# Waits between the four scatter rounds of the expert stages, on GpSimd's queue

## What is computed

```
x = x + attn_a(layernorm(x))      # state-space heads, 32 of them
x = x + ffn(layernorm(x))         # shared expert + 16 experts, top 4
x = x + attn_b(layernorm(x))      # gated linear attention, 16 heads
x = x + ffn(layernorm(x))         # the same weights again
```

```
shared = silu_and_mul(x @ shared_gate_up_w.T) @ shared_down_w.T
shared = shared * sigmoid(x @ sgate_w.T)
routing_weights = softmax(x @ gate_w.T)
topk_w, topk_ids = top_k(routing_weights, 4)
for e in range(16):
    coef = sum(where(topk_ids == e, topk_w, 0), axis=-1)
    h = silu_and_mul(x @ w13[e].T)          # 2 x 176 hidden columns
    acc = acc + (h @ w2[e].T) * coef[:, None]
out = shared + acc
```

## Time and profile before

| | us |
|---|---|
| runs, median of 3 | 1252.41 (1249.12 to 1254.31) |
| the profiled execution, its own time | 1253.93 |
| its span, first to last instruction | 1252.0 |
| TensorE matmul busy | 1175.0 (94%) |
| VectorE busy | 807.0 (64%) |
| ScalarE busy | 752.3 (60%) |
| GpSimd busy | 600.4 (48%) |
| scatters (L1285), 64 | 63.9 busy |
| scatter-adds (L1291), 88 | 137.6 busy |

### The profile page before, as it was taken

How to read it: one execution, slowest core, us unless ns; L and a number is a source line. 1 busy time by engine, 2 the same in 40 slices (tenths; PEclk the granted TensorE clock), 3 DMA queues, 4 the chain that set the end, 5 groups by cost and what they waited for, 6 DMA issues and landing times.

```text
span 1252.0 us, 23038 instructions
## 1 busy us (share of the span) xinstructions
PE 1175.0 (94%) x7484; PEld 1008.6 (81%) x7484; DVE 807.0 (64%) x2038; ACT 752.3 (60%) x1734; POOL 600.4 (48%) x497
## 2 busy tenths in 40 slices
PE   6999999999897899989999999999999989489997
PEld 5878888888784777768999999999999988377775
DVE  7766767777882433477777777777777787143335
ACT  5866667666551333427888887887888865033332
POOL 3211222121137165625776777677776643705663
PEclk9999999999997899989999999999999998789999
DMA  3366766653245777741322222232222015556665
GB/s 114 88 181 169 175 174 174 170 162 71 58 153 203 181 137 137 129 103 51 89 77 59 59 61 65 61 70 79 59 75 59 17 48 158 201 168 112 117 116 145
DMA packets 94277, 141.59 MB, mean 113 GB/s; under 512 B 8184, under 2 KB 73976, under 8 KB 93048
## 3 DMA queue, kind: packets, MB, share of 16 engines
q1 hardware_dynamic: 74400, 102.32, 29.8%
q0 software_dynamic: 15744, 20.98, 9.8%
q10 hardware_dynamic: 4056, 17.30, 4.6%
HBM read 99.71 MB, written 40.86 MB: 112 GB/s over the span
## 4 chain that ended last, share of the span: by engine, by line
PE 80%; DVE 6%; DMA 6%; issue 4%; ACT 2%; POOL 1%; SPq 0%; DVEq 0%; ACTq 0%; POOLq 0%
PE ps L276 20%; PE ps L278 19%; PE ps L277 19%; PE ps L1116 7%; PE ps L1141 5%; DMA sums_d<-e_y,xg 3%; PE ps L551 2%; DMA rows_a<-a_rows_d 1%; PE ps L1129 1%; PE ps L1093 1%; DVE valT L762 1%; PE ps L1680 1%; PE ps L565 1%; DMA a_vg_raw<-a_vg 1%; DVE x L1419 1%
## 5 line engine op out<-in xcount | busy, mean ns | idle before, releaser
L1291 POOL DMA_INDIRECT sums_d<-e_y,xg x88 | 137.6, 1564 | 137.2 <-ACT e_y L1218 79.8
L1116 PE MATMUL ps<-w,e_xT 128*128 (+1 forms) x376 | 127.2, 461 | 2.5 <-ACT e_xT L1201 1.7
L1412 DVE COPY e_hT<-ps 88x256 f32<-88x256 f32 x94 | 39.5, 420 | 132.0 <-PE ps L1129 118.0
L427 POOL TENSOR_TENSOR aw_lo<-aw_raw,aw_hi 128x512 fp32r<-128x512 f32 x32 | 42.0, 1317 | 152.5 <-ACT aw_hi L423 152.5
L276 PE MATMUL ps<-xn_hi,aw_hi 128*128 128x512 f32 x256 | 111.2, 434 | 2.7 <-DVE bmat_lo L790 2.7
L857 DVE TENSOR_TENSOR m_a<-ps,e_a 128x384 f32<-128x384 f32 x128 | 71.3, 557 | 58.5 <-PE ps L551 57.9
L278 PE MATMUL ps<-xn_hi,aw_lo 128*128 128x512 f32 x256 | 101.4, 396 | 0.0
L277 PE MATMUL ps<-xn_lo,aw_hi 128*128 128x512 f32 x256 | 100.9, 394 | 0.0
L1141 PE MATMUL ps<-w,e_hT 88*128 (+1 forms) x376 | 96.7, 379 | 0.0
L656 ACT COPY late<-ps 128x256 f32<-128x256 f32 x128 | 47.7, 373 | 69.7 <-PE ps L278 69.6
L427 POOL TENSOR_TENSOR ms_b_lo<-m_b,ms_b_hi 128x384 fp32r<-128x384 f32 x64 | 65.0, 1017 | 49.2 <-ACT ms_b_hi L423 49.2
(11 more groups left out here) (311 smaller groups left out, 4145.8 us busy)
## 6 DMA issues: line engine op xcount, KB each, us to landing
rows_a<-a_rows_d SPq DMA_DIRECT2D x64, 256.0 KB, 5.1
xg<-slots_d SPq DMA_DIRECT2D x94, 144.0 KB
slots_d<-slot_init SPq DMA_DIRECT2D x10, 1152.0 KB, 6.9
w<-moe_up ACTq DMA_DIRECT2D x8, 1408.0 KB
wconv_raw<-b_conv SPq DMA_DIRECT2D x16, 513.0 KB
aw_raw<-a_heads SPq DMA_DIRECT2D x32, 256.0 KB, 3.0
wvo_raw<-b_vo SPq DMA_DIRECT2D x16, 512.0 KB, 3.4
rows_b<-b_rows_d SPq DMA_DIRECT2D x32, 256.0 KB, 4.8
```

The source lines that it names most:

```text
L427: return nc.gpsimd.tensor_tensor(dst[1], src, f32(dst[0]), ALU.subtract).then_inc(sem(done_sem), 1)
L1116: ins = nc.tensor.matmul(ps[:, 2 + t % 2, 0:2 * E_HIDDEN], e_xT[:, t % 2, k], weights_of(w13, t, at_w, k * 2 * E_HIDDEN, 2 * E_HIDDEN), st ...
L1291: nc.gpsimd.indirect_dma_start(sums_d[f][t % CHAINS], bass.IndirectOffsetOnAxis(ap=xg[:, t % XG, ROW_ID:ROW_ID + 1].bitcast(U32), axis=0), ...
L1412: nc.vector.tensor_copy(e_hT[0:HALF_E, t % 2], ps[0:HALF_E, 4 + t % 2, 0:2 * P].rearrange("p (j m) -> p j m", j=2)).then_inc(sem("e_hT"), 1)
```

## The change

In both expert stages GpSimd waits, ahead of each round after the first, until all eight scatters of the round before have landed.

```diff
             for i, k in enumerate(reversed(range(TOP_K))):
+                if i > 0:
+                    pool.wait_ge(sem(f"slots_stored{i - 1}"), 16 * BLOCKS * (f + 1))
                 for b in range(BLOCKS):
                     if i == 0 and b % CHUNK_BLOCKS == 0:
                         routed(pool, "dve", f, f"slots{b // CHUNK_BLOCKS}")
```

## The result

| | before | after |
|---|---|---|
| runs beside each other, median of 11 each, us | 1252.41 | 1243.15 |
| ratio of after to before, 95% interval | | 0.9929 [0.9909, 0.9949] |
| the profiled execution, its own time, us | 1253.93 | 1240.95 |
| its span, us | 1252.0 | 1239.1 |

Faster, by 0.7%: 9 us by the runs, 13.0 us between the two profiled executions. The forecast was a gain of 18.5 us, to 1234 us.

The account below looks back on a forecast made before the run. TensorE's slow instruction flow during unbroken scatter bursts was taken as the bound. Tile 3 earlier by 7.5 + 15 us, less 4 for the clock, gives 18.5; 1253.9 - 18.5 - 1.5 = 1234 us, eight-in-ten range 1225 to 1260.

Parts of the forecast that it names:

- The slow stretches and their cure: Both expert stages, 25 and 28 us of slow matmuls inside the scatter burst: bursts of eight end them; chance 0.52, 1234 us.
- tile 3 waits for its load: Sign in the profile after: tile 3's turn waits for its load, at 418 to 423 and 1105 to 1110.
- The rival that the slow pace stays: TensorE is slowed by scatters under way, not their number in a row; stretches end 6.1 us later, 1262 us; chance 0.19.
- no change: Rival: pauses put off the slow pace's onset by about what they lengthen the burst; 1247 to 1258 us; chance 0.18.
- The price of the waits: GpSimd's three waits per stage: 3.7, 1.2 and 1.2 us added, 6.1 us in all, up to 4.5 more for weights.
- the forecast's own sum: Tile 3 starts earlier by 7.5 and 15 us in the two stages, less 4 for the clock: 18.5 us gained.
- 4 us for the clock: TensorE's clock falls while it waits for tile 3; a loss of 2 us per stage was taken.
- half a cure: Rival: slow pace returns in the last choices, or weight loads hold scatters up beyond the bounds; 1238 to 1247 us; chance 0.11.
- the rule that engines take their queues in turn: DMA engines alternate queues packet by packet, so full scatter queues shut nothing out; if that is all, the slower rival's time.
- The load of a tile with nothing beside it: Tile 3's load of 144 KB, once the scatters have landed: estimated at 2.2 us.

## Why the prediction was right on the cure and wrong on its price

**The slow stretches and their cure: right.** Bursts of eight keep TensorE's pace, "issue" is gone, the waits are put down to the scatters' landing, tile 3 waits for its load. TensorE reaches the first tile at 402.72, where before it turned it at 424.2: 21.5 us sooner, forecast 22. In the second stage it is 27 us (1118.8 to 1086.80, less 4.8 that the stage starts earlier), forecast 25. The rival that the slow pace stays is out; so is "no change".

**The price of the waits: the step that failed.** I put the first wait at 4 us, the other two at 1.49 us, and 0 to 4.5 us more for weights, over these two and the last landing: the load of tile 3 was to go out at 415.8 to 420.3. It went out at 422.57, 12.9 us later than in the earlier trace rows; in the second stage 13.9 us later, measured from the first scatter. The waits took 6.16, 6.90 and 1.73 us. 14.8 less the three usual gaps of 0.30 is 13.9 us of cost against the 6.1 to 10.6 us of the forecast. Put into the forecast's own sum it gives tile 3 at 409.7 + 13.9 + 2.2 = 425.8 and 1113.0, gains of 2.2 and 9.6 us where the forecast had 7.5 and 15. The profile has 3.3 us and, less the 4.8 us of the earlier start, 9.6 us: together the 13.0 us between the two profiled executions. So this one term accounts for the miss. (Less its 4 us for the clock, the sum so put right is some 8 us, near the 9 us of the runs, but that is luck: in the profile those 4 us don't show.) What happened is one branch of the rival that I called half a cure (weights that hold the scatters up beyond my bounds, 1238 to 1247) and gave 0.11.

Where I chose wrongly: for the first wait the rows had 5.3 and 7.4 us as upper ends, which SP's view of the same landing gave, and I took less. For the second I saw that TensorE, set free, would let the next weights go out inside the burst, and still gave it 1.49 to 3 us, less than the first, though the same 2 MB would fall on the same eight scatters. The runs show that each wait costs what the weights in it make it: 6.9 to 1.7 and 1.7 to 8.2 us when they were moved, 6.2 to 3.4 when the first was relieved.

I weighed the rule that engines take their queues in turn only as saying that the scatters are not shut out; that each turn of the weights delays them is the price that I left out. The Trainium skill has another rule by which weights lengthen a landing wait ("DMA: Bandwidth & Descriptors", Queues, rings and completion order): the increment of the semaphore that tells of a landing is ordered behind every earlier write of its DMA engine, those of other queues too. The trace leaves little to that rule here: of the 5.2 us by which the second wait is longer than the third, 0.3 us lie behind the last packet of rows. No run tests it by itself.

**Smaller terms.** The load of a tile with nothing beside it took 2.1 us from issue to turn (422.57 to 424.71, 1106.02 to 1108.19), as estimated (2.2). Tile 1's, beside weights, took 8.0 us (399.08 to 407.08). The clock loss of 2 us per stage can't be told apart: between tile 3 and the next stage 1.5 us more were gained in the first, 1.5 us given back in the second.

**What stays open.** The two profiled executions differ by 13.0 us, the runs by 9: the one of before lies 1.5 us above its median, that of after 2.2 us below. What sets this spread I have no row for. And what it is that fills up was not found.

## What to carry to other kernels

A wait for a landing cost here what else was in the DMA engines at that moment, so price it by the traffic that will be there after the change, not before it, and if the wait is only for pacing, pace with something that doesn't depend on a landing. Where an engine stalls under "issue", look at what another engine does without a break in just that time, and test it with a pause before looking for a dependency. Bulk loads that hide behind a paced stage can cost more in the loop that follows.

## What was unexpected

In an unbroken run of scatters TensorE doesn't only slow down: what it signals comes out late. It shows in the kernel before already, where I had read ScalarE as merely short of work. `f_down_weights_act` (L1260) waits for six ends of the shared expert's second product; the sixth is the last L278 here. TensorE's timeline, then ScalarE's, before:

```profile
386.04 0.28 PE L278 MATMUL ps<-fd_hi,fh_lo 128*128 128x256 f32 x1
...
387.85 0.60 ACT L1234 ACTIVATE f_s<-ps 128x512 f32<-128x512 f32 x1 [3.70 <-remote]
...
411.73 0.41 ACT L423 CAST fd_hi<-fw_raw 128x256 fp32r<-128x256 f32 x1 [20.80 <-remote]
```

The product ended at 386.32 and ScalarE went on at 411.73, 25.4 us later, 2.0 us behind SP's release by the last scatter. So "remote" beside a long wait was a lead that I passed over.

The trace also holds the time of each semaphore's update, which settles that it was the signal that came late, and not ScalarE. The last four of the six ended at 375.84, 377.28, 384.88 and 386.32, and their updates stand at 375.86, 377.82, 398.37 and 411.70: 0.02, 0.5, 13.5 and 25.4 us late. Those of VectorE and ScalarE that stand in the trace between 366 and 416 come 0.01 or 0.02 us behind their ends. In this stage the lateness thus begins at the ninth scatter (377.24), when TensorE still runs at full pace, and the pace falls some seven scatters later. With the change, those updates of this semaphore and of the first product's that stand in the trace are at most 0.7 us late in both bursts. By this order the late signals may be what brings the pace down, but no run shows it. With single clears between the scatters ScalarE has no wait on "remote" in either burst.

After 13 to 17 scatters in a row, at one every 1.2 to 1.3 us, the slow pace began in every run without breaks, whatever the weights, the rows per scatter or the place in TensorE's program. It ended 2 to 5 us behind the landing of the last.
